# Mixture of 32 experts: the down product turned around, in three passes of rounded halves, with a lag of three units

## The reference, cut to what matters

```python
x = x + _L1_ffn_ref(_layernorm(x, axis=-1), ...)
...
logits = flat @ gate_w.T
scores = jax.nn.sigmoid(logits)
topk_w, topk_i = _group_topk(scores)          # 4 of 8 groups of 4 experts, then 8 experts
topk_w = topk_w / jnp.clip(topk_w.sum(axis=-1, keepdims=True), 1e-12)
combine = jnp.zeros((T, E), flat.dtype).at[jnp.arange(T)[:, None], topk_i].add(topk_w)

def body(acc, expert):
    wg, wu, wd, w = expert                    # I = 64 hidden features each
    h = jax.nn.silu(flat @ wg.T) * (flat @ wu.T)
    return (acc + w[:, None] * (h @ wd.T), None)
out, _ = jax.lax.scan(body, jnp.zeros_like(flat), (expert_gate, expert_up, expert_down, combine.T))
shared = jax.nn.silu(flat @ shared_gate_w.T) * (flat @ shared_up_w.T) @ shared_down_w.T
out = out + shared
```

## Time and profile before

| | |
|---|---|
| median of 3 runs | 2665.84 us (2662.67 to 2671.37) |
| the profiled execution, its own time | 2661.88 us |
| its span | 2660.1 us |
| TensorE's granted clock, mean | 0.966 |
| first `up` of the stage to the end | from 2324.0 us |
| PE busy, DVE busy, ACT busy, POOL busy, share of the span | 93%, 61%, 53%, 39% |

### The profile page before, as it was taken

How to read it: one execution, slowest core, us unless ns; L and a number is a source line. 1 busy time by engine, 2 the same in 40 slices (tenths; PEclk the granted TensorE clock), 3 DMA queues, 4 the chain that set the end, 5 groups by cost and what they waited for, 6 DMA issues and landing times. The chain is left out here.

```text
span 2660.1 us, 92957 instructions
## 1 busy us (share of the span) xinstructions
PE 2482.2 (93%) x38497; PEld 2096.3 (79%) x38497; DVE 1610.0 (61%) x3115; ACT 1418.8 (53%) x3839; POOL 1049.4 (39%) x1152
## 2 busy tenths in 40 slices
PE   6999999999989999997679998999999989889999
PEld 5888888888877888885469986777777768778888
DVE  3555555555567777775655554777777747544553
ACT  3555555555556667674644444777777734422222
POOL 2333333333340000002344444666666623345555
PEclk9999999999999999998869998999999989789999
DMA  6322222222134111110020000210101010065563
GB/s 201 128 89 89 89 89 89 89 89 89 67 125 170 40 47 39 47 40 2 1 71 1 0 0 23 50 30 24 30 24 30 13 52 0 3 135 111 107 136 75
DMA packets 60190, 168.35 MB, mean 63 GB/s; under 512 B 6429, under 2 KB 20385, under 8 KB 55209
## 3 DMA queue, kind: packets, MB, share of 16 engines
q1 hardware_dynamic: 60074, 166.71, 21.2%
HBM read 145.18 MB, written 21.51 MB: 63 GB/s over the span
## 5 line engine op out<-in xcount | busy, mean ns | idle before, releaser
L566 POOL TENSOR_TENSOR l_probs<-l_probs,l_rden 128x1024 f32<-128x1024 f32 x128 | 242.2, 1892 | 428.8 <-DVE l_rden L424 428.8
L508 ACT ACTIVATE l_probs<-ps,l_nmax 128x257 f32<-128x257 f32 x512 | 236.0, 474 | 226.4 <-DVE l_nmax L418 226.4
L967 POOL TENSOR_TENSOR l_probs<-l_probs,l_rden 128x1024 f32<-128x1024 f32 x128 | 242.3, 1893 | 171.2 <-DVE l_rden L818 171.2
L418 DVE TENSOR_REDUCE l_nmax<-ps 128x2 f32<-128x514 f32 x256 | 165.5, 688 | 217.4 <-PE ps L303 217.4
L903 ACT ACTIVATE l_probs<-ps,l_nmax 128x257 f32<-128x257 f32 x512 | 236.0, 474 | 59.9 <-DVE l_nmax L812 59.9
L2723 POOL TENSOR_TENSOR m_hh<-m_hh,m_cb 128x512 f32<-128x512 f32 (+1 forms) x136 | 177.3, 1304 | 156.6 <-DVE m_hh L2675 138.5
L303 PE MATMUL ps<-l_ctxQ,l_q 32*128 32x257 f32 x3072 | 202.6, 392 | 7.1 <-ACT l_probs L508 6.4
L2581 ACT ACTIVATE m_sg<-ps 128x512 f32<-128x512 f32 (+1 forms) x136 | 81.3, 598 | 231.6 <-PE ps L138 230.8
L812 DVE TENSOR_REDUCE l_nmax<-ps 128x2 f32<-128x514 f32 x256 | 165.4, 688 | 61.1 <-PE ps L704 57.6
L2675 DVE TENSOR_TENSOR m_hh<-ps,m_sg 128x512 f32<-128x512 f32 (+1 forms) x136 | 94.0, 691 | 178.6 <-PE ps L138 159.0
L823 DVE COPY l_pT<-ps 128x512 f32<-128x512 f32 x256 | 164.9, 686 | 52.2 <-PE ps L713 48.0
(11 more groups left out here) (371 smaller groups left out, 6471.1 us busy)
## 6 DMA issues: line engine op xcount, KB each, us to landing
l_ctxQ<-in_ctx_q SPq DMA_DIRECT2D x32, 1542.0 KB, 6.5
m_cb<-combined SPq DMA_DIRECT2D x32, 768.0 KB, 13.8
enc_dash<-kept SPq DMA_DIRECT2D x32, 512.0 KB, 3.3
l_ctxT<-in_ctx_t SPq DMA_DIRECT2D x32, 385.5 KB, 3.3
l_ctxK<-in_ctx_k SPq DMA_DIRECT2D x32, 384.0 KB, 3.1
m_cb<-combined SPq DMA_DIRECT2D x16, 512.0 KB, 13.5
kept<-enc_va SPq DMA_DIRECT2D x10, 512.0 KB, 3.2
kept<-enc_qsq SPq DMA_DIRECT2D x6, 512.0 KB
```

Source lines behind the costliest of these rows:

```text
L418: nc.vector.tensor_reduce(nmax[:, par, 2 * half:2 * half + 2], ps[:, S_B + 2 * half:S_B + 2 * half + 2, 0:NK], AX.X, ALU.max, negate=True) ...
L508: nc.scalar.activation(probs[:, par, hg, :], ps[:, S_B + hg, 0:NK], ACT.Exp, bias=nmax[:, par, hg:hg + 1], accum_out=den[:, par, hg:hg + 1 ...
L566: nc.gpsimd.tensor_tensor(pr, pr, rden[:, b, :, None].to_broadcast([P, HG, NK - 1]), ALU.mult).then_inc(norm_ok, 1)
L967: nc.gpsimd.tensor_tensor(pr, pr, rden[:, b, :, None].to_broadcast([P, HG, K_W]), ALU.mult).then_inc(norm_ok, 1)
```

## The change

- `down` now has features on the output's partitions: wd as the stationary operand, hh (128x512) as the moving one, in three fp32r passes (high times high, high times low, low times high), summed into one bank of 128x512.
- So hh has to be split into a rounded high and a low half. ACT's new `high` copies hh to the high half; DVE's new `remains` subtracts it from hh for the low half. Both stand one unit behind, after silu(v) and DVE's up(v). wd is split once, by a copy on ACT and a subtraction on POOL before unit 0.
- The sums have to be turned back per group: ACT's new `sums_out` (at c = 4 of the next group) copies the bank to SBUF, PE's new `turn_out` (c = 6) does four transposes, and DVE's `out` moves from c = 2 to c = 7.
- The lag on PE is three units in place of two.
- hh, sg, xn4, gt and eq now lie in the buffers wg and wu, whose weights are used up by then (so their names in a trace are m_wg and m_wu; the halves are m_parts, the split wd is m_down_w).

```diff
-    NV, TURN_AT, LAG = NG * NCH, 10, 2
+    NV, TURN_AT, LAG, OUT_AT = NG * NCH, 10, 3, 6
...
             def down(v, g, c):
                 rows = rows_of(c)
-                pe.wait_ge(h_ok, v + 1)
+                if v == 0:
+                    pe.wait_ge(wd_lo, 1)
                 if c == 0 and g > 1:
-                    pe.wait_ge(x_ok, g - 1)
+                    pe.wait_ge(to_ok, g - 1)
+                pe.wait_ge(lo_ok, v + 1)
+                pe.nop(nofuse=True)
+                out = ps[:, ACC + g % 2, :]
+                hi, lo = [parts[0:rows, v % 3, n, :] for n in range(2)]
+                nc.tensor.matmul(out, down_w[0:rows, 0, c, :], hi, start=c == 0, stop=False)
+                nc.tensor.matmul(out, down_w[0:rows, 0, c, :], lo, start=False, stop=False)
+                nc.tensor.matmul(out, down_w[0:rows, 1, c, :], hi, start=False, stop=c == NCH - 1).then_inc(dn_mm, 1)
+
+            def turn_out(g):
+                pe.wait_ge(to_ok, g + 1)
+                if g:
+                    pe.wait_ge(x_ok, g)
                 pe.nop(nofuse=True)
                 for n in range(4):
-                    last = nc.tensor.matmul(ps[:, ACC + g % 2, n * P:n * P + D], hh[0:rows, v % 3, n * P:n * P + P],
-                                            wd[0:rows, c, :], start=c + n == 0, stop=c == NCH - 1 and n == 3)
-                last.then_inc(dn_mm, 1)
+                    last = nc.tensor.transpose(ps[:, OUT_B, n * P:n * P + P], turned_out[:, n * P:n * P + P], k.ident[:, :])
+                last.then_inc(to_mm, 1)
...
+                if c == OUT_AT and g:
+                    turn_out(g - 1)
                 if c == TURN_AT and g < NG - 1:
                     turn_combined(g + 1)
             for v, g, c in units[NV - LAG:]:
                 down(v, g, c)
+            turn_out(NG - 1)
...
+            def high(v, g, c):
+                rows = rows_of(c)
+                act.wait_ge(h_ok, v + 1)
+                if v > 2:
+                    act.wait_ge(dn_mm, v - 2)
+                nc.scalar.copy(parts[0:rows, v % 3, 0, :], hh[0:rows, v % 3, :]).then_inc(hi_ok, 1)
+
+            def sums_out(g):
+                act.wait_ge(dn_mm, NCH * g + NCH)
+                if g:
+                    act.wait_ge(to_mm, g)
+                nc.scalar.copy(turned_out[:, :], ps[:, ACC + g % 2, :]).then_inc(to_ok, 1)
...
+            nc.scalar.copy(down_w[:, 0, :, :], wd[:, :, :]).then_inc(wd_hi, 1)
             for v, g, c in units:
                 silu(v, g, c)
+                if v:
+                    high(*units[v - 1])
+                if c == OUT_AT - 2 and g:
+                    sums_out(g - 1)
...
                 if v > 2:
-                    dve.wait_ge(dn_mm, v - 2)
+                    dve.wait_ge(hi_ok, v - 2)
+                    dve.wait_ge(lo_ok, v - 2)
...
+            def remains(v, g, c):
+                rows = rows_of(c)
+                dve.wait_ge(hi_ok, v + 1)
+                nc.vector.tensor_tensor(parts[0:rows, v % 3, 1, :], hh[0:rows, v % 3, :],
+                                        parts[0:rows, v % 3, 0, :].bitcast(F32), ALU.subtract).then_inc(lo_ok, 1)
+
             def out(g):
-                dve.wait_ge(dn_mm, NCH * g + NCH)
+                dve.wait_ge(to_mm, g + 1)
...
             for v, g, c in units:
                 up(v, g, c)
-                if c == LAG and g:
+                if v:
+                    remains(*units[v - 1])
+                if c == OUT_AT + 1 and g:
                     out(g - 1)
                 if c < 10 and g < NG - 1:
                     rank(g + 1, c)
+            remains(*units[NV - 1])
             out(NG - 1)
...
+            pool.wait_ge(wd_hi, 1)
+            nc.gpsimd.tensor_tensor(down_w[:, 1, :, :], wd[:, :, :], down_w[:, 0, :, :].bitcast(F32),
+                                    ALU.subtract).then_inc(wd_lo, 1)
             for v, g, c in units:
                 weigh(v, g, c)
```

More of the change, by code:

```diff
@@ L2417, in stage_moe1 @@
         wd, wide, gate, lower = [bufs[n] for n in ("wd", "wide", "gate", "lower")]
+        free_a, free_b = bufs["wg"], bufs["wu"]
+        hh = free_a[:, 0:1536].rearrange("p (r n) -> p r n", r=3)
+        sg = free_b[:, 0:1024].rearrange("p (r n) -> p r n", r=2)
+        turned_out = free_b[:, 1024:1536]
+        gt, eq = [free_b[:, n:n + 256].rearrange("p (t a b) -> p t a b", t=4, a=8) for n in (1536, 1792)]
+        xn4 = free_a[:, 0:1024].rearrange("p (r t d) -> p r t d", r=2, t=4)
         xs = sbr("xs", [P, T, 2, P])
-        xn4, xf4 = sb("xn4", [P, 2, 4, D]), sb("xf4", [P, 2, 4, P])
+        xf4 = sb("xf4", [P, 2, 4, P])
         shift = sb("shift", [P, T])
@@ L2424, in stage_moe1 @@
         tot = sb("tot", [P, 4])
-        gt, eq = sb("gt", [P, 4, 8, 8]), sb("eq", [P, 4, 8, 8])
         comb, ct, cb = sb("comb", [P, T, NX]), sb("ct", [NX, 512]), sb("cb", [P, NCH, 512])
-        sg, hh = sb("sg", [P, 2, 512]), sb("hh", [P, 3, 512])
+        parts, down_w = sbr("parts", [P, 3, 2, 512]), sbr("down_w", [P, 2, NCH, D])
         (ln, sh_ok, xv_ok, xa_ok, xt_mm, xf_ok, xh_ok, xl_ok, lg_mm, sg_sc, ones_ok, rk) = [sem(n) for n in (
@@ L2431, in stage_moe1 @@
             "g_mm u_mm sg_ok hh_ok h_ok dn_mm cb_ok ct_mm ct_ok ct_out x_ok stored").split()]
+        hi_ok, lo_ok, wd_hi, wd_lo, to_ok, to_mm = [sem(n) for n in "hi_ok lo_ok wd_hi wd_lo to_ok to_mm".split()]
         back = [sem(f"back{n}") for n in range(len(BLOCKS))]
-        GU_B, CT_B, ACC = 0, 4, 6
+        GU_B, CT_B, OUT_B, ACC = 0, 4, 5, 6
         X_B, L_B = 0, 2
@@ L2593, in _ @@
             combined_out(0)
+            nc.scalar.copy(down_w[:, 0, :, :], wd[:, :, :]).then_inc(wd_hi, 1)
             for v, g, c in units:
                 silu(v, g, c)
+                if v:
+                    high(*units[v - 1])
+                if c == OUT_AT - 2 and g:
+                    sums_out(g - 1)
                 if c == TURN_AT and g < NG - 1:
                     combined_out(g + 1)
+            high(*units[NV - 1])
+            sums_out(NG - 1)
         @block.vector
@@ L2673, in up @@
                 if v > 2:
-                    dve.wait_ge(dn_mm, v - 2)
+                    dve.wait_ge(hi_ok, v - 2)
+                    dve.wait_ge(lo_ok, v - 2)
                 nc.vector.tensor_tensor(hh[0:rows, v % 3, :], ps[0:rows, GU_B + 2 * (v % 2) + 1, :], sg[0:rows, v % 2, :],
                                         ALU.mult).then_inc(hh_ok, 1)
+            def remains(v, g, c):
[3 more added lines that the diff above has]
+                                        parts[0:rows, v % 3, 0, :].bitcast(F32), ALU.subtract).then_inc(lo_ok, 1)
             def out(g):
-                dve.wait_ge(dn_mm, NCH * g + NCH)
+                dve.wait_ge(to_mm, g + 1)
                 xg = k.x[:, 4 * g:4 * g + 4, :]
-                nc.vector.tensor_tensor(xg, ps[:, ACC + g % 2, :].rearrange("p (t d) -> p t d", t=4), xg,
+                nc.vector.tensor_tensor(xg, ps[:, OUT_B, :].rearrange("p (t d) -> p t d", t=4), xg,
                                         ALU.add).then_inc(x_ok, 1)
```

## The result

The changed kernel takes 2679.6 us (median of 8 runs, 2675.4 to 2684.2) against 2668.8 us before (8 runs, 2662.7 to 2673.2). The ratio is 1.0042, with a 95% interval of 1.0029 to 1.0054: slower by 11 us, where 27 us had been forecast. The profiled execution has a span of 2676.9.

What follows compares the result with a forecast made beforehand. TensorE was taken to bound the kernel before, with DVE and POOL's turns filling their spare time after. Terms 15.6 - 3.2 + 2 + 2.6 + 10 gave +27 us on the 2665.8 median: 2693 us, range 2664 to 2714.

Steps and rivals of the forecast that it cites:

- the ranked groups: The seven groups with rank parts: each 2.2 us longer, +15.6 us in all.
- the start: Start of the stage: DVE's third multiplication queues behind unit 0's subtraction, so one unit's chain is not prepared, +2 us.
- the clock: TensorE's granted clock falls after the idle time at the combine weights' turn, in four groups of seven: +10 us.
- the last group and the end: Last group without rank parts at TensorE's pace, -3.2 us; longer chain after the last multiplication, +2.6 us.
- What bounds the kernel, and the mechanism: The stage runs at TensorE's pace; DVE operations with two SBUF operands and POOL take turns, filling their spare time.
- The gain on TensorE: Three passes replace four fp32 matmuls: a unit takes 2.07 us, a group 36.4 in place of 39.6 if TensorE sets the pace.
- just ready in time: In units with a rank part, the subtraction's input is ready when DVE reaches it: 3.4 us against 2.67 + 0.61.
- Nine units at 2.67, eight at 2.07 ... +2.2: Per group, nine units slowed by turns plus eight at TensorE's pace: 41.9 us against 39.6, +2.2.
- the fall after 2278 to 2280: Before the change, PE was busy 0.36 of 2 us, then the granted clock went to 0.50; basis for expected falls.
- The hold of 0.53: In DVE and POOL's turns, the subtraction holds POOL off for 0.53 us, less than its record of 0.69.
- Serialised, but the clock holds: Rival: DVE and POOL take turns but TensorE's clock does not fall; +17 us, 2683 us, chance 0.22.
- The late spreads: Rival: weight spreads reach POOL late, with 0.3 us left to spare; at most a few us, no chance of its own.

Runs made afterwards that it cites:

- e5: The changed kernel with the split of hh left out after the first three units, the turned product kept: 2643.5 us, ratio 0.9928 to the kernel before.
- e2: The changed kernel with DVE's subtraction taking its first operand from a PSUM bank of zeros instead of hh in SBUF: 2651.4 us, ratio 0.9953.
- e6: The changed kernel with DVE's subtraction two units behind the multiplication instead of one, and a lag of four: 2662.5 us, ratio 0.9981.
- e11: The changed kernel run again without edits: 2679.3 us, ratio 1.0052 to the kernel before.
- e9: The kernel of e7 with later rank parts and the turn of the combine weights one unit earlier: 2654.8 us, ratio 0.9950 to the kernel before.
- e8: The changed kernel with only POOL's weighing made to wait for rank parts with two SBUF operands: 2699.7 us, ratio 1.0129 to the kernel before.
- e10: The same kernel as e7, run again: 2646.9 us, ratio 0.9934 to the kernel before.
- e7: The changed kernel with e6's edits and POOL's weighing waiting for rank parts with two SBUF operands: 2653.3 us, ratio 0.9952 to the kernel before.

## Why the prediction was right in kind and wrong in size

The sum was +27 and the profiles show +10.7. Set side by side, the ranked groups and the start were put at 15.6 + 2 = 17.6 and measured 9.5, of which 1.6 is a fall of the clock and 7.9 theirs; the clock was put at 10 and measured 1.6 there; the last group and the end were put at -0.6 and measured +1.2. Two steps failed, of about the same size: the clock (8.4 too much) and the groups with the start (9.7 too much).

*What bounds the kernel, and the mechanism: right, with one part missing.* The gain on TensorE is there (e5: 36.66, forecast 36.4), and the turns between DVE and POOL take it and more (e2). A multiplication every 2.61 in the first ten units makes 26.1; nine at 2.67 and one at 2.07 had also made 26.1. That they agree is luck. The prediction called the subtraction "just ready in time (3.4 against 2.67 + 0.61)", but the sum is 3.28, so it is late by 0.1, and in a plain unit it is late too (2.9 against 2.07 + 0.61 = 2.68). Late, it falls into POOL's next weighing, and that is what the wait for the high half shows, 35 times in some 100 units. With the half in time (e6) the first ten units take 24.4: without the late half the forecast of 26.1 would have been 1.7 a group too high.

*"Nine units at 2.67, eight at 2.07 ... +2.2": a step that failed, a term too large.* I added 0.44 + 0.44 + 0.36 us of turns and 64-row loads on TensorE to a group that DVE and POOL set the pace of. They lie in TensorE's idle time: the seven units from c = 10 on take 14.76, not 7 x 2.07 + 1.24 = 15.7. Measured: +1.3 a group. This is read from the spacings; no run takes those small terms away.

*Start, "+2": not there.* From the first store to the second, which holds the start and one ranked group, I had 2 + 2.2 and it was +0.2; in e11 that interval is 39.03, 0.1 less than before. POOL's first weighing comes 14.2 us after the store, 14.6 before, and the second interval is longer only by the fall of the clock. Why the unprepared chain costs nothing is not shown.

*TensorE's clock, "+10": the other step that failed.* I took a fall of 5 us at half clock, 2.5 us dear, in four groups of seven. Measured: one fall in seven turns, 3.4 us long, worth 1.6 us, and in e11 again one in seven. I had carried over the fall after 2278 to 2280 by the length of the gap alone. The length does not decide: of fourteen gaps of 2.02 to 2.04 us in one and the same list of matmuls, two lowered the clock and twelve did not. What does decide, no run here shows. The rule of the Trainium skill's "TensorE: Matmul & The Clock Gate", section "HAM oscillation — how this bites in real kernels", told of a wait at each tile that brings the low clock each time; here the wait came back in each group and brought it once.

*Last group and end, -3.2 + 2.6 = -0.6: measured +1.2.* The last multiplication starts at 2666.26 and the last addition at 2673.50, 7.2 against 3.3 before, +3.9 in place of +2.6. Part of it is the clock, which is 0.81 in the mean of the last 17 us (the row of 2660 to 2677 above). The timeline at the end of the changed kernel:

```profile
2670.19 0.57 PE L2526 MATMUL ps<-m_parts,m_down_w 64*128 64x512 f32 x1 [1.57 <-DVE m_parts L2723]
2670.56 0.62 PE L2527 MATMUL ps<-m_parts,m_down_w 64*128 64x512 f32 x1
2670.98 0.62 PE L2528 MATMUL ps<-m_parts,m_down_w 64*128 64x512 f32 x1
2671.64 0.58 ACT L2615 COPY m_wu<-ps 128x512 f32<-128x512 f32 x1 [2.32 <-PE ps L2528]
2672.38 1.09 PE L2536 MATMUL ps<-ident,m_wu 128*128 128x128 f32 x4 [0.77 <-ACT m_wu L2615]
```

Passes 0.37 and 0.42 apart and a turn of 1.09 are the lower level, about 0.5 us each beyond what I had counted.

*The hold of 0.53: right.* At 2507.02 a subtraction starts (record 0.67) and POOL's weighing, recorded from 2507.17, takes 1.67 in place of 1.30 by the first 0.37: POOL was held until 2507.54, 0.52 after the subtraction's start and 0.15 before its record ends. The Trainium skill ("SBUF — State Buffer", section "SBUF: two separate sides") says that the turns are exclusive and that the first comer holds the pair for its whole instruction. The rows shown agree with the first; by the second the hold would have been the 0.67 of the record, and the row shows 0.52.

*The rivals.* "Serialised, but the clock holds" came nearest, at +17 in my sum and +11 in fact, one fall included. The late spreads appeared in the faster kernels, and by e9 they cost nothing there.

## What to carry to other kernels

An engine that is idle half the time need not have room: ask what it shares, and with whom, and count the turns in one unit from start to start. Where two engines take turns at SBUF, order them by hand: make the operand early enough to be always ready (one unit more of lag), and let the long operation wait for the short one that something stands behind. Here the first alone gained less (e6) and the second alone lost (e8). And when an engine stops being the bound, leave its small terms out of the sum.

## What the runs showed of the hardware that I had not expected

- The turns do not go by who came first. POOL waited from 2511.72 behind the subtraction, and L2664, issued at 2512.17, went in ahead of it; in the earlier trace rows the second of two DVE operations, issued as closely, did not. The weighings of 2.00 us in place of 1.30 are of this kind.
- A gap of 2.03 us on TensorE left the granted clock at 1.00 twelve times and lowered it to 0.50 twice, with the same matmuls before it. A fall cost 1.6 us in a group of the change, and 1.1 to 1.4 in one of e8.
- The first store of weights, up to which all these kernels have the same code ahead of the stage, comes anywhere from 2321.1 (e10) to 2339.1 (e6) in single profiles. A difference of 11 us in one pair of spans would have said little. The store-to-store times of the change from the second interval on repeat within 0.1, but for the 42.50 and for e11's last, 41.21, whose 0.3 is not explained; those of e7 and e10, one kernel, spread from 37.40 to 37.85, and once to 38.70.
